# Moving the shared expert out of the per-tile loop of a mixture-of-experts kernel, and the weight check to the end of the first attention

## The reference

```
x = x + LN(attention0(LN(x)))        # 16 heads of 8, softmax over blocks of 64 keys
x = x + LN(ternary_mlp(LN(x)))       # 128 -> 512 -> 512 -> 512 -> 128
x = x + LN(attention1(LN(x)))        # FFT-style heads, cumulative sum over the tokens
x = x + LN(experts(LN(x)))

experts(x):
    shared = (silu(x @ sg.T) * (x @ su.T)) @ sd.T
    logits = x @ gate_w.T;  top_id = argmax(logits);  score = sigmoid(max(logits))
    xs = x * score
    routed = sum over e of swiglu(where(top_id == e, xs, 0), e)     # 8 experts, hidden size 256
    return shared + routed
```

## Time and profile before

| | |
|---|---|
| median of three runs | 1793.39 us (1789.89 to 1798.41) |
| profiled execution, its own time | 1789.92 us |
| its span, first to last instruction | 1788.0 us |
| PE / DVE / ACT / POOL busy over the span | 89 / 74 / 64 / 40 % |
| mean granted clock of PE | 0.941 of 2.4 GHz |

### The profile page before, as it was taken

One profiled execution on the slowest core, in us unless ns is written; L12 is line 12 of the kernel. 1 busy time (PEld: TensorE's weight loads), 2 busy tenths in 40 slices (PEclk: granted clock), 3 DMA queues, 4 the chain that ended last, 5 costly groups with the idle time before them and its releaser, 6 DMA issues. The chain is left out here.

```text
span 1788.0 us, 35516 instructions
## 1 busy us (share of the span) xinstructions
PE 1583.6 (89%) x8576; PEld 874.2 (49%) x8577; DVE 1328.3 (74%) x3585; ACT 1147.1 (64%) x2294; POOL 712.2 (40%) x1011
## 2 busy tenths in 40 slices
PE   4999999999999999999499999999498973899996
PEld 2333333333333333333277777777345542566664
DVE  5899999999999999997256666666357763466664
ACT  1587888888888888888366666666236553343342
POOL 2224343434444434222413333333135776244444
PEclk7799999999999999999699999999799985899998
DMA  5333223323222233210100000000120113222210
GB/s 129 82 90 100 85 81 95 90 72 94 84 83 85 82 88 85 84 54 22 45 32 1 1 0 0 0 0 1 32 68 18 46 47 107 62 59 61 57 55 17
DMA packets 84447, 102.50 MB, mean 57 GB/s; under 512 B 15995, under 2 KB 49537, under 8 KB 84368
## 3 DMA queue, kind: packets, MB, share of 16 engines
q1 hardware_dynamic: 78992, 88.89, 17.9%
q0 software_dynamic: 5376, 12.66, 2.1%
HBM read 61.44 MB, written 35.33 MB: 54 GB/s over the span
## 5 line engine op out<-in xcount | busy, mean ns | idle before, releaser
L836 DVE TENSOR_REDUCE bmax<-PS 128x8 f32<-128x512 f32 x1024 | 651.5, 683 | 53.7 <-PE PS L577 51.1
L689 ACT ACTIVATE EX<-PS 128x512 f32<-128x512 f32 x1024 | 565.2, 604 | 106.2 <-PE PS L588 96.5
L577 PE MATMUL PS<-KR,QR 33*128 33x512 f32 x1024 | 411.0, 469 | 43.2 <-DVE bmax L836 30.9
L588 PE MATMUL PS<-QR,KR 64*128 64x512 f32 x1024 | 399.0, 460 | 1.6 <-ACT EX L689 1.5
L577 PEld LDWEIGHTS PS<-KR,QR 33*128 33x128 f32 x1024 | 166.9, 188 | 358.8 <-DVE bmax L836 298.3
L598 PE MATMUL PS<-EX,VS 128*9 128x512 f32 x2048 | 267.9, 595 | 1.2 <-ACT EX L689 1.2
L588 PEld LDWEIGHTS PS<-QR,KR 64*128 64x128 f32 x1024 | 162.4, 185 | 11.3 <-ACT EX L689 10.2
L1035 PE MATMUL PS<-pA,wb 128*128 128x512 f32 x640 | 157.4, 402 | 0.0
L774 POOL TENSOR_TENSOR m_diff<-m_prev,m_all 128x16 f32<-128x16 f32 x64 | 14.2, 223 | 326.9 <-DVE m_all L848 326.9
L1864 ACT ACTIVATE g<-PS 128x512 f32<-128x512 f32 x72 | 43.0, 597 | 142.9 <-PE PS L1824 142.9
L1035 PEld LDWEIGHTS PS<-pA,wb 128*128 128x128 f32 x640 | 120.7, 192 | 27.5
(11 more groups left out here) (227 smaller groups left out, 2829.7 us busy)
## 6 DMA issues: line engine op xcount, KB each, us to landing
QR<-q_scr SPq DMA_DIRECT2D x256, 64.0 KB, 2.4
KR<-k_scr SPq DMA_DIRECT2D x256, 64.0 KB, 2.3
k_scr<-partsB SPq DMA_DIRECT2D x42, 256.0 KB, 2.9
rows<-row_scr SPq DMA_DIRECT2D x72, 129.0 KB, 2.1
q_scr<-partsB SPq DMA_DIRECT2D x28, 256.0 KB, 3.0
X<-in_L_attn_x SPq DMA_DIRECT2D x16, 256.0 KB, 3.0
X<-x SPq DMA_DIRECT2D x16, 256.0 KB, 2.4
xB<-in_L_attn_x SPq DMA_DIRECT2D x14, 256.0 KB, 3.3
```

The costliest lines, as they stand in the source:

```text
L577: pe.matmul(PS[:, bank_of(i, n), :], QR[rows, i, h // 2, t * P:(t + 1) * P], KR[rows, i, h // 2, :], start=True, stop=True).then_inc(tile_ ...
L588: pe.matmul(PS[:, RING3 + bank_of(j, n), :], KR[rows, j, h // 2, kt * P:(kt + 1) * P], QR[rows, j, h // 2, :], start=True, stop=True).then ...
L689: act.activation(EX[:, n % (2 * HG), :], PS[:, RING3 + bank_of(j, n), :], ACT.Exp, scale=SCALE).then_inc(ex_set, 1)
L836: dve.tensor_reduce(bmax[:, i % 2, n, :], PS[:, bank_of(i, n), :].rearrange("p (b k) -> p b k", k=BLK), AX_X, ALU.max).then_inc(tile_max, 1)
```

## The change

The weight check moves. `w_raw` now holds all eleven pieces; SP loads them together when the last two chunks of the first attention begin, POOL rounds two of them in each of the next groups, and DVE compares them in the four steps behind the last score group. The MLP block loads no weights of its own.

The shared expert leaves the per-tile loop. It is computed once per chunk of 512 tokens in a new stage `shared` with lag 17 (`SHARED_LAG`), behind the second attention of all chunks, from the transposed normalised rows, which are now kept for all chunks in `XT`. A row in `row_scr` now holds three pieces of 128: the normalised row already multiplied by its score, the shared expert's result, and the residual row, then the token's number (`ROW` 385 numbers in place of 258). `assemble` and `scatter` go with that stage. The scores are taken in two batches.

The expert stage is now in the same block, fully written out (`tile_steps`), and computes the chosen expert alone. The shared result enters the sum by one matmul with the identity. ACT normalises in place of DVE, and four banks take the results in place of two.

```diff
-                if isinstance(g, int) and g < NWB:
-                    load_weights(g)
+                if isinstance(g, int) and g == ENDING * NG:
+                    for n in range(NWB):
+                        load_weights(n)
...
-                if isinstance(g, int) and g < NWB:
-                    cast_weights(g)
+                if isinstance(g, int):
+                    for n in range(NWB):
+                        if g == ENDING * NG + 1 + n // 2:
+                            cast_weights(n)
...
-                if isinstance(g, int) and 1 <= g <= NWB:
-                    check_weights(g - 1)
+                if isinstance(g, int):
+                    for n in range(NWB):
+                        if g == GROUPS + n // 3:
+                            check_weights(n)
...
+            def shared_in(c):                     # PE
+                pe.wait_ge(xT4_set, c + 1)
+                for f in range(FB1):
...
+                    pe.matmul(PS[:, 1 + 2 * f, :], sgu[:, f * P:(f + 1) * P], chunk_of(XT, c), start=True, stop=True)
+                    pe.matmul(PS[:, 2 + 2 * f, :], sgu[:, F1 + f * P:F1 + (f + 1) * P], chunk_of(XT, c),
+                              start=True, stop=True).then_inc(gus_done, 1)
+            def shared_rows(c):                   # PE
...
+                for t in range(NT):
+                    for f in range(FB1):
+                        mm = pe.matmul(PS[:, 5, t * P:(t + 1) * P], hs[:, c % 2, f, t * P:(t + 1) * P],
+                                       sdn[:, f, :], start=(f == 0), stop=(f == FB1 - 1))
...
+            def assemble(c):                      # ACT
+                s = c % 2
+                if c >= 2:
+                    act.wait_ge(row_out[s], (c - s) * 32)
+                act.wait_ge(ys_done, c + 1)
+                act.copy(row[:, s, :, E:2 * E], ...)
...
+                for t in range(NT):
+                    n = c * NT + t
+                    act.activation(row[:, s, t, 0:E], tile_of(AO, c, t), ACT.Identity,
+                                   scale=score[:, n:n + 1]).then_inc(row_set, 1)
...
-            run_stages(pool, NCH, [(3, lambda c, s: rstd(ln4)(pool, c)), (1, spectra),
-                                   (2, lambda c, s: rstd(lnC)(pool, c)), (7, scatter)])
+            run_stages(pool, NCH, [(3, lambda c, s: rstd(ln4)(pool, c)), (1, spectra),
+                                   (2, lambda c, s: rstd(lnC)(pool, c))])
+            for c in range(NCH):
+                scatter(c, c % 2)
...
+            def load(j):                          # SP
+                r = sp.value_load(tile_row[0:1, j:j + 1], min_val=0, max_val=NE * REGION)
+                if j >= RING:                     # RING = 10
+                    sp.wait_ge(o7_set, j - RING + 1)
+                sp.dma_start(rows7[:, j % RING, :], row_scr[ds(r, P)]).then_inc(row_in[j % RING], 16)
...
+            tile_steps([(0, turn_x), (3, turn_h), (4, reduce), (1, expand), (0, next expert)])          # PE
+            tile_steps([(7, normalise), (0, copy_xT7), (3, copy_hT), (1, silus)])                       # ACT
+            tile_steps([(5, inverse_std), (8, scatter_out)])                                            # POOL
+            tile_steps([(8, add_residual), (2, gate), (6, bias7), (5, stats), (0, take_idx)])           # DVE
```

More of the change, by code:

```diff
@@ L377, in block_kernel @@
         ln2 = ln_bufs("ln2", p2, LN_SPLIT)
[L378 removed]
         w_diff = sb("w_diff", [P, S], F32, p2)
[L380 removed]
+        w_raw_in = sem("w_raw_in")
         w_cast = sem("w_cast")
@@ L1414, in block_kernel, with tile_steps @@
         RB = 7
+        HELD = 6
+        SHARED_LAG = NCH + 1
+        EARLY = NCH // 2
+        idx7 = sb("idx7", [P, ST_TILES], U32, p5)
+        xT7 = sb("xT7", [P, 2, P], F32, p5)
+        g7 = sb("g7", [P, 2, F1], F32, p5)
+        h7 = sb("h7", [P, 2, F1], F32, p5)
+        hT7 = sb("hT7", [P, 2, FB1, P], F32, p5)
+        st7 = sb("st7", [P, 2, 6], F32, p5)
+        mv7 = sb("mv7", [P, 4, 2], F32, p5)
+        ve7 = sb("ve7", [P, 4], F32, p5)
+        rs7 = sb("rs7", [P, 4], F32, p5)
+        nb7 = sb("nb7", [P, 4], F32, p5)
+        o7 = csum[:].rearrange("p a (b e) -> p (a b) e", e=E)
+        gs = kA
+        hs = qq
+        row_in = [sem(f"row_in{k}") for k in range(RING)]
+        score_set = sem("score_set")
+        idx7_set = sem("idx7_set")
+        turned7 = sem("turned7")
+        xT7_set = sem("xT7_set")
+        gu7_done = sem("gu7_done")
+        g7_set = sem("g7_set")
+        h7_set = sem("h7_set")
+        h7_turned = sem("h7_turned")
+        hT7_set = sem("hT7_set")
+        y7_done = sem("y7_done")
+        st7_set = sem("st7_set")
+        ve7_set = sem("ve7_set")
+        rs7_set = sem("rs7_set")
+        nb7_set = sem("nb7_set")
+        n7_set = sem("n7_set")
+        o7_set = sem("o7_set")
+        o7_out = [sem(f"o7_out{k}") for k in range(HELD)]
+        gus_done = sem("gus_done")
+        gs_set = sem("gs_set")
+        hs_set = sem("hs_set")
+        ys_done = sem("ys_done")
+        out_rows = out.rearrange("b s e -> (b s) e")
+        ROUTE = 16
+        X_BANK, H_BANK, Y_BANKS, GU_BANKS = 0, 1, (2, 3, 4, 5), (6, 7)
+        def tile_steps(stages):
+            last = max(lag for lag, _ in stages)
+            for i in range(ST_TILES + last):
+                for lag, stage in stages:
+                    if 0 <= i - lag < ST_TILES:
+                        stage(i - lag)
         with nc.Block() as block:
@@ new lines, in shared, with expert @@
+                def shared(c, s):
+                    if c == 0:
+                        pe.wait_ge(w8_in, 96)
+                    shared_in(c)
+                    if c:
+                        shared_rows(c - 1)
+                run_stages(pe, NCH, [(0, project), (6, ranks), (4, turn), (1, combine), (2, output), (5, logits),
+                                     (SHARED_LAG, shared)])
+                shared_rows(NCH - 1)
+                experts = {}
+                def expert(j):
+                    experts[j] = pe.value_load(tile_e[0:1, j:j + 1], min_val=0, max_val=NE - 1)
@@ new lines, in turn_x, with expand @@
+                def turn_x(j):
+                    pe.wait_ge(row_in[j % RING], j // RING * 16 + 16)
+                    if j:
+                        pe.wait_ge(xT7_set, j)
+                    pe.transpose(PS[:, X_BANK, 0:P], rows7[:, j % RING, 0:E], idf[:]).then_inc(turned7, 1)
+                def expand(j):
+                    s = j % 2
+                    pe.wait_ge(xT7_set, j + 1)
+                    if j >= 2:
+                        pe.wait_ge(h7_set, j - 1)
+                    pe.matmul(PS[:, GU_BANKS[s], :], xT7[:, s, :], wgu[:, ds(experts[j] * (2 * F1), 2 * F1)],
+                              start=True, stop=True).then_inc(gu7_done, 1)
@@ new lines, in _, with copy_xT7, silus @@
+                assemble(NCH - 1)
+                def copy_xT7(j):
+                    act.wait_ge(turned7, j + 1)
+                    if j >= 2:
+                        act.wait_ge(gu7_done, j - 1)
+                    act.copy(xT7[:, j % 2, :], PS[:, X_BANK, 0:P]).then_inc(xT7_set, 1)
+                def silus(j):
+                    s = j % 2
+                    act.wait_ge(gu7_done, j + 1)
+                    if j >= 2:
+                        act.wait_ge(h7_set, j - 1)
+                    act.activation(g7[:, s, :], PS[:, GU_BANKS[s], 0:F1], ACT.Silu).then_inc(g7_set, 1)
```

456 lines of the change are left out of this document (207 added, 249 removed).

## The result

The changed kernel takes 1738.09 us (median of 4 runs, 1737.36 to 1741.15), the kernel before, on the same chip, 1792.72 us. The ratio is 0.9713, 95% interval 0.9695 to 0.9731: 3% faster (the two medians alone divide to 0.9695). The forecast was 1739 us in 1710 to 1772. The profiled execution has a span of 1735.6 us and took 1.8 us more in all; the forecast span was 1735.7.

The account below looks back on a forecast made before the run. PE bound the expert stage at 3.34 us a tile; a routing chain was waited for ahead of it. First load 1575.6 + expert stage 169.6 - check 9.5 = 1735.7 us span; with 1.9 and 3.5 added, forecast 1739, range 1710 to 1772.

Parts of the forecast that it names:

- The check: First attention: moving the weight comparisons off DVE's score groups gains 9.5 us, bounds 7 to 10.3; new place costed at 0.
- whose work feeds transposes that wait for an engine anyway: End of first attention: the comparisons fit in DVE's idle gaps and cost 0, up to 2 us without that cover.
- The loop: Second attention: without ACT's `assemble` pieces, eleven iterations take 9.9 us instead of 11.4, gaining 16.6 us, bounds 12 to 18.
- The shared stage: Shared expert per chunk: six mixed iterations about 53 us, 7, nine of 5.4, then 1.8; 110 us, bounds 100 to 122.
- To the first load: After the shared stage: last `assemble` 3.1, three scatter spacings 3.8, landing 2.6, SP 0.5 us until the first row load.
- The expert stage: Chosen expert's tiles: 72 of 2.05 us plus 22 for fill and drain, 169.6 us, against 263.5 before.
- T = 2.05: Time per expert-stage tile in us, from PE 1.90 and POOL 1.90 to 2.14 plus a little; bounds 1.90 and 2.5.
- contention: Rival, expert stage: DVE's two-input operations wait for POOL over SBUF ports, T = 2.45, 29 us more, 1768 us; chance 0.12.
- The tail as a chain: Rival: six mixed iterations cost 11 us each and scatters hold shared chunks at 6.2, giving 1759 us; chance 0.17.
- rows did not come late: Rival, expert stage: row landings of 5.1 us or more make T 2.95, 65 us more, 1804 us; chance 0.03.
- the loop was bound by `kA`: Second attention: PE's wait for ACT's `kA` sets iterations; rival, another wait binds, 17 us stay away, 1756 us, chance 0.09.
- Everything overlaps: Rival: T = 1.90 us a tile and the shared stage at 100 us, giving 1718 us; chance 0.14.

Follow-up runs that it names:

- kernel 1: The changed kernel with the weight check's loads, casts and comparisons put back among the first eleven groups, one a group: 1745.69 us, ratio 0.9767.
- experiments 1 to 3: Changed kernel with the whole weight check back early (1745.69 us); only loads and casts early (1736.05); the same with two comparisons a step, not three (1737.62).
- experiment 8: The changed kernel with ACT's four old row pieces written again in the second attention's loop for chunks 0 to 9, without scatters: 1749.53 us, ratio 0.9767.
- experiment 10: The changed kernel with two shared chunks a step in the first five mixed iterations, then one a step: 1741.53 us, ratio 0.9719.
- experiment 9: The changed kernel with three row buffers instead of two between ACT and the row scatters: 1738.67 us, ratio 0.9704.
- experiment 4: The changed kernel without PE's identity product, so the output lacks the shared expert: 1751.33 us in one run; repeated on another chip, 1736.82 us.
- the experiment with both: The changed kernel without PE's identity product and with POOL's inverse deviation computed for every second tile only: 1.715 us a tile on the mean, 1743.33 us.

## Why the prediction was right, and where its terms were off

- **The check, -9.5.** The gain at the old place was 9.6 (744.13 in the changed kernel against 753.71). The new place was costed at 0, with 2 for lost cover. The tail is 2.9 longer than in the kernel before, of which 2.2 come from the comparisons (50.80 against 48.64 in kernel 1). The other 0.7 stands in kernel 1 too: PE's transposes of `xn` take 1.1 us there and in the changed kernel, 0.66 in the kernel before, in a stretch where the granted clock falls (from 862 to 870 us it is 0.61 on the mean in kernel 1, 0.71 in the kernel before). The burst of loads cost 0.7 to 1.3. Net: -5.1 to -7.0 against the kernel before at the end of the attention, and 6.7 to 8.5 by the traces of experiment 1. The step that failed is "whose work feeds transposes that wait for an engine anyway": DVE's gaps were long enough, but POOL's work beside them was stretched, which the prediction held to be a matter of the expert stage alone (experiments 1 to 3).
- **The loop, -16.6.** Measured -15.8 (9.98 an iteration for 9.9). Right in size, and in mechanism by experiment 8, which gives back 13.6 of them.
- **The shared stage, 110 us.** 113.4 from 1448.85 to 1562.2: the first six iterations took 58.1 for 53 and the seventh 5.3 for 7, nine chunks 5.22 us for 5.4, the last products 3.0 for 1.8. In the later part PE and POOL are side by side as forecast: PE passes a chunk every 5.22 us, and POOL's scatters, 5.12 for four on the mean, hardly pause from 1516.51 on. The mixed iterations are chains through ACT, which experiment 10 could not shorten. The prediction priced PE in them at full clock; the three chunks at the lower clock took 5.5 us more than that for their wide products, about what the six iterations are over. No run separated this from the waits.
- **To the first load, 10.0 us.** Measured 13.1 (1562.2 to 1575.35). The sum took `assemble` and four scatters one behind the other; but POOL still had the scatters of the chunk before in its queue when the last rows were full, and the last landing and the load's issue took 3.7 us for 3.1. Experiment 9 shows that a buffer more does not help; the queue is what is left.
- **The first load** thus went out at 1575.35 and not at 1566.1: +9.3, of which 3.4 and 3.1 are from the two steps above and 2.8 from what stands before the first mixed iteration: 4.4 from the check and 0.8 from the loop, less 2.5 that the prediction did not have, half between the check and the loop and half behind the loop.
- **The expert stage, 169.6 us.** Measured 160.2: 72 x 1.86 = 133.9 and 26.3 for fill, drain and the pauses, where I had 147.6 and 22. T = 2.05 was mis-sized: I took for the gap behind a scatter a share of the 0.30 that stands between two scatters, and added "a little" for four engines handing on. Behind a scatter another operation of POOL follows after some hundredths of a microsecond, so that POOL's two terms, 0.81 + 1.03 = 1.84, stood without a gap. The hand-overs cost nothing that the trace shows, with PE busy 98.98 of 100 us; that four banks and a ring of ten absorb them was not tested. PE's sum of 1.90 was right to 0.04. POOL's cycle, where it catches up, is 1.08 from scatter to power and 0.76 from power to scatter, 1.84; experiment 4 gives 1.83. The Trainium skill (Perfetto Trace Analysis, section GPSIMD Engine Instruction) says to go by such spacings and not by spans; the trace agrees, since the spans of the two, 1.03 + 0.58, would give 1.61.
- **Rivals.** No contention shows in the expert stage: DVE's residual add takes 0.28 us beside POOL's power at 0.59 (0.57 in the earlier trace rows), and T is 1.86, not 2.45. By the page's rule the two contend; for operations this short the trace has at most 0.02 us of it. A stretch of that kind showed where I had not looked. The tail as a chain came true in part (9.7 us for each of the first six iterations, not 11, and no 6.2 behind them), rows did not come late (a load of 192.5 KB landed in 2.4 us), and the loop was bound by `kA`. "Everything overlaps" was right for T and wrong for the stage ahead of it.
- **The sum.** 1739 does not follow from its own terms: 1735.7 + 1.9 + 3.5 is 1741.1. The measured median stands 0.7 above the profiled execution, not 3.5. So the nearness of 1738.09 to 1739 is luck as well.

## What to carry to other kernels

When work is moved into an engine's idle time, ask what its work does to the neighbour's beside it: 2.2 us were lost on POOL with 3 to 5 us of idle time left on DVE, the engine that got the work. When two engines stand within a few hundredths of a microsecond (PE 1.86, POOL 1.83), relieving one of them shows nothing; only the experiment with both tells what lies below. And a stage moved one iteration later must have its waits derived anew: one release taken from the old consumer closed a ring over two engines and turned a gain of 10 us that was hoped for into a loss of 40.

## What the runs showed of the hardware

- POOL takes 1.265 us from one indirect scatter's start to the next of its kind, but an inverse deviation behind a scatter starts 1.07 us after the scatter's start: the 0.30 between two scatters is not there in front of a tensor operation.
- DVE's comparisons of two SBUF tiles stretch POOL's scalings from 3.14 to 3.88 us and its power from 1.03 to 1.48; beside the adds of 0.28 us in the expert stage its power takes 0.59, against 0.57 in the kernel before.
- In single executions of three kernels on one chip, in code that they share with the changed kernel, ACT paused about 2.3 and 3.8 us again and again, every 20.5 us in kernel 4, with nothing on the core to release it. In 8 timed runs of the changed kernel this cost appeared in none.
- TensorE ran at the lower of its two levels (granted clock 0.50) from 1464 to 1470 us, after 6 us in which it was busy 3.69, and two of its wide products then took 2.05 us in place of 1.02.
